# A Trainium2 graph-convolution kernel: embeddings and features of later images through the gather's idle PSUM banks, by halves

## The reference

```python
xn = _gn(x)                                # statistics, then (x - m) / sqrt(v + eps)
emb = einsum('bnc,ec->bne', xn, dist_w)    # 32 numbers per pixel
d2 = sq[:, :, None] + sq[:, None, :] - 2 * einsum('bne,bme->bnm', emb, emb)   # sq: sum of emb squared
adj = (24 nearest by d2) & (dist <= 10) | eye         # 1024 x 1024 zeros and ones
X_lin = xn @ fc_w.T + fc_b                            # features
Dv = sum(adj, axis=2); De = sum(adj, axis=1)
S = (adj / De) @ adj.T / Dv
out = S @ X_lin + xn
o = batchnorm(out)                          # statistics over all four images
result = x + o * sigmoid(o)
```

## Time and profile before

| quantity | value |
|---|---|
| median of 3 runs | 205.23 us (205.18 to 209.13) |
| profiled execution, its own time | 205.92 us |
| its span in the trace | 203.8 us |
| busy share of the span: PE, DVE, ACT, POOL | 87%, 77%, 58%, 42% |
| granted TensorE clock, mean | 0.949 |

### The profile page before, as it was taken

How to read it: one execution, slowest core, us unless ns; L and a number is a source line. 1 busy time by engine, 2 the same in 40 slices (tenths; PEclk the granted TensorE clock), 3 DMA queues, 4 the chain that set the end, 5 groups by cost and what they waited for, 6 DMA issues and landing times.

```text
span 203.8 us, 4396 instructions
## 1 busy us (share of the span) xinstructions
PE 177.9 (87%) x1338; PEld 100.7 (49%) x1338; DVE 156.1 (77%) x912; ACT 118.9 (58%) x207; POOL 85.2 (42%) x120
## 2 busy tenths in 40 slices
PE   7999988889999959999899969999986999999400
PEld 2336352236547636545366645555564577757300
DVE  1789959779998549985995098999999873695664
ACT  2157779687687869637656697444485322060192
POOL 1004821469424169932060689845226751320000
PEclk9999999579999996999999999999999999999955
DMA  5801000155327426422293642442442199610038
GB/s 168 305 5 1 2 3 0 9 99 101 58 54 89 64 6 128 84 53 51 52 60 49 53 106 53 82 77 51 53 56 51 10 125 223 85 30 0 0 115 298
DMA packets 44404, 14.83 MB, mean 73 GB/s; under 512 B 41813, under 2 KB 42453, under 8 KB 44378
## 3 DMA queue, kind: packets, MB, share of 16 engines
q1 hardware_dynamic: 43514, 14.14, 39.4%
q10 hardware_dynamic: 864, 0.40, 0.7%
HBM read 4.02 MB, written 2.13 MB: 30 GB/s over the span
## 4 chain that ended last, share of the span: by engine, by line
PE 36%; DVE 24%; issue 13%; DMA 8%; POOL 8%; ACT 7%; DVEq 2%; SPq 1%; ACTq 0%; POOLq 0%
DVE cand L790 9%; PE pg L366 8%; PE pt L391 7%; PE po L410 6%; PE pt L410 5%; DMA inv_rows<-rdv 5%; POOL H L697 4%; PE pt L431 4%; DVE top L805 3%; DVE cwork L810 3%; DMA dvb<-inv_rows 3%; DVEq L829 2%; DVE xn L992 2%; DVE prod L904 2%; PE pg L343 1%
## 5 line engine op out<-in xcount | busy, mean ns | idle before, releaser
L790 DVE MAX8 cand<-key 128x8 f32<-128x64 f32 x512 | 81.2, 210 | 2.0 <-ACT key L568 1.2
L391 PEld LDWEIGHTS pt<-xp,H 128*128 128x128 bf16 x768 | 45.7, 99 | 22.1 <-issue 14.9
L391 PE MATMUL pt<-xp,H 128*128 128x128 bf16 (+1 forms) x768 | 50.6, 223 | 2.4 <-issue 2.0
L568 ACT ACTIVATE key<-pg 128x512 f32<-128x512 f32 x64 | 35.0, 593 | 26.0 <-PE pg L366 26.0
L366 PE MATMUL pg<-right,left 64*128 64x512 f32 x128 | 47.3, 675 | 3.0 <-ACT key L568 1.4
L576 ACT ACTIVATE sign<-key,thr 128x1024 bf16<-128x1024 f32 x32 | 36.7, 1146 | 11.9 <-DVE thr L816 11.9
L692 POOL TENSOR_SCALAR low<-cs 128x1 f32<-128x1 f32 x32 | 6.0, 187 | 69.7 <-ACT sign L576 66.9
L410 PE MATMUL po<-HT,tp 128*128 128x512 bf16 x144 | 34.0, 380 | 1.1 <-ACT tp L589 0.7
L697 POOL TENSOR_SCALAR H<-sign 128x1024 bf16<-128x1024 bf16 x32 | 33.4, 1043 | 2.5
L366 PEld LDWEIGHTS pg<-right,left 64*128 64x128 f32 x128 | 14.0, 192 | 17.6 <-issue 8.8
L410 PEld LDWEIGHTS po<-HT,tp 128*128 128x128 bf16 x144 | 12.7, 98 | 15.1 <-ACT tp L589 1.2
(11 more groups left out here) (91 smaller groups left out, 199.2 us busy)
## 6 DMA issues: line engine op xcount, KB each, us to landing
out<-xn SPq DMA_DIRECT2D x7, 256.0 KB, 2.1
dvb<-inv_rows SPq DMA_DIRECT2D x3, 512.0 KB, 5.7
x_sb<-x SPq DMA_DIRECT2D x1, 1024.0 KB, 6.2
x_sb<-x SPq DMA_DIRECT2D x1, 512.0 KB, 3.7
HT<-H SPq DMA_TRANSPOSE x32, 3.2
x_sb<-x ACTq DMA_DIRECT2D x1, 256.0 KB, 3.2
x_sb<-x SPq DMA_DIRECT2D x1, 256.0 KB, 3.6
out<-xn SPq DMA_DIRECT2D x2, 128.0 KB, 2.5
```

The costliest lines, as they stand in the source:

```text
L391: mm = pe.matmul(pt[:, j // T_BLOCKS, at:at + wide], lhs, x_cols(b, t, q, wide), start=(t == 0 and j % T_BLOCKS == 0 and q == 0), stop=(t ...
L568: act.activation(key[:, k % KEYS, cols], pg[:, h, :], ACT.Copy).then_inc(s["drained"], 1)
L790: ins = dve.max(cand[:, k % 2, c, :], key[:, k % KEYS, c * CHUNK:(c + 1) * CHUNK])
```

## The change

1. Embeddings and features of images 1 and 2 and the embedding of image 3 (and features of image 0) go through `po` instead of `pg`, with an order of their own (`po_pair`, semaphores `po_filled`, `po_drained`). Features of image 3 stay in `pg`. The embeddings go in steps 0, 5 and 10 (were 1, 6 and 14), their squares' sums in the step behind, `operands` half by half in steps +1 and +2. Features go by halves in steps 3 and 4 (were: 1), 8 and 9 (were: 9) and, image 3's, both in 18 (were: 17).
2. The middle piece of the features moves from ACT to POOL; POOL makes the three pieces of a half in one go (`x_pieces`).
3. The key fill stands first in every step, except t = 3 of images 1 to 3, where the scatter goes first.
4. `gather` of images 0 to 2 goes by piece, then part; it waits for `po_drained` of image 3's embedding. The last image's share of gather(2) is (12, 14, 14, 8) instead of (12, 14, 12, 10).
5. `out_part` moves from t = 7 and t = 4 to t = 1 and t = 2 of the image behind; the statistics `y_stats` of images 0 and 1 move behind the loop: three ahead of the last tile's flag, one behind the last `scale_t`.
6. In the head the statistics of image 2 go behind the operands, those of image 3 behind `candidates(0)`; candidates(0) starts on the first drained half; the group steps of images 2 and 3 move a step later on every engine.

The pieces of the diff stand in the order of the file: tables and `build`, then the loop of PE, the loop of ACT, `x_pieces` on POOL, and DVE.

```diff
+EMB_STEPS = {0: 1, 5: 2, 10: 3}
+X_STEPS = {3: [(1, 0)], 4: [(1, 1)], 8: [(2, 0)], 9: [(2, 1)], 18: [(3, 0), (3, 1)]}
+        po_pair = {("emb", 0): 0, ("x", 0): 1, ("emb", 1): 2, ("x", 1): 3, ("emb", 2): 4, ("x", 2): 5, ("emb", 3): 6}
+        def x_bank(b, h):
+            return (po if ("x", b) in po_pair else pg)[:, h, :]
-                GATHER[b, t] = (b - 1, (12, 14, 12, 10)[t - T_STEP] if b == B - 1 else 8)
+                GATHER[b, t] = (b - 1, (12, 14, 14, 8)[t - T_STEP] if b == B - 1 else 8)
...
+            def gather_order(b):
+                n = len(parts(b))
+                if b == B - 1:
+                    return [(part, q) for part in range(n) for q in range(PIECES)]
+                return [(part, q) for q in range(PIECES) for part in range(n)]
...
+                    if q == 0 and j == 0 and b == 0:
+                        pe.wait_ge(s["po_drained"], 2 * po_pair["emb", B - 1] + part + 1)
...
+                    if b > 0 and t == LAG:
+                        for kk in settled:
+                            scatter(kk)
+                    if k + AHEAD < ALL:
+                        fill_key((k + AHEAD) // TILES, (k + AHEAD) % TILES)
+                    if not (b > 0 and t == LAG):
+                        for kk in settled:
+                            scatter(kk)
+                    if k in EMB_STEPS:
+                        embed(EMB_STEPS[k])
+                    if k - 1 in EMB_STEPS:
+                        norms(EMB_STEPS[k - 1])
+                    for bb, h in X_STEPS.get(k, []):
+                        fill_x(bb, h)
                     if k > 0:
                         flag(k - 1)
+                    if k == 1:
+                        group_variances(2, 2, B)
                     if (b, t) in GATHER:
                         gather(*GATHER[b, t])
...
                     if k > 0:
                         mark(k - 1)
+                    if k == 2:
                         group_sd(2, 2, B)
+                    if k - 2 in EMB_STEPS:
+                        operands(EMB_STEPS[k - 2], 1)
                     if b > 0 and t == T_STEP:
                         t_high(b - 1)
                     if b > 0 and t == T_STEP + 1:
                         t_middle(b - 1)
+                    if k + AHEAD < ALL:
+                        drain_key((k + AHEAD) // TILES, (k + AHEAD) % TILES)
+                    if k in EMB_STEPS:
+                        squares(EMB_STEPS[k])
+                    if k - 1 in EMB_STEPS:
+                        operands(EMB_STEPS[k - 1], 0)
+                    for bb, h in X_STEPS.get(k, []):
+                        drain_x(bb, h)
...
+            def x_pieces(b, h):
+                pool.wait_ge(s["x_hi"], 4 * b + 2 * h + 2)
+                pool.tensor_tensor(x_tiles(xr32, h), x_tiles(x32, h), x_piece(b, h, 0), ALU.subtract)\
+                    .then_inc(s["x_res"], 1)
+                pool.wait_ge(s["x_res"], 2 * b + h + 1)
+                pool.tensor_copy(x_piece(b, h, 1), x_tiles(xr32, h)).then_inc(s["x_mid"], 1)
+                pool.wait_ge(s["x_mid"], 2 * b + h + 1)
+                pool.tensor_tensor(x_piece(b, h, 2), x_tiles(xr32, h), x_piece(b, h, 1), ALU.subtract)\
+                    .then_inc(s["x_lo"], 1)
...
+            dve.wait_ge(s["x_in23"], 16)
+            group_stats(2, 3)
+            group_inverse(1, 1, 2)
+            candidates(0, range(CHUNKS))
             dve.wait_ge(s["step"], group_stats(3, B))
             group_moments(2, B)
...
+                    if b > 1 and t == 1:
+                        out_part(b - 2, 0)
+                    if b > 1 and t == 2:
+                        out_part(b - 2, 1)
...
+            out_part(B - 2, 0)
+            for h in range(2):
+                y_stats(0, h)
+            y_stats(1, 0)
             for k in RELEASE[ALL]:
                 read_flag(k)
                 release(k)
...
             split_last_t(B - 1)
+            y_stats(1, 1)
```

More of the change, by code:

```diff
@@ L182, in build @@
         g_sums = [misc, misc, pt[:, 0, :]]
-        def emb_bank(b, h):
-            return (pg if b > 0 else po)[:, h, :]
         block = ctx.enter_context(nc.Block())
-        first_pairs = [("key", 0, 0), ("key", 0, 1), ("x", 0, 0), ("key", 0, 2), ("key", 0, 3)]
+        first_pairs = [("key", 0, t) for t in range(AHEAD)]
         def pairs_of_step(b, t):
@@ L284, in _ @@
                         inverse_in(b - 1)
[L285 to L288, removed]
+                    for step, image in EMB_STEPS.items():
+                        if image > 1 and b * TILES + t == step + 2 - LAG:
+                            norms_out(image)
+                        if image > 1 and b * TILES + t == step + 3 - LAG:
+                            norms_in(image)
                     if t == TILES - 1 and b < B - 1:
@@ L321, in embed @@
                         pe.wait_ge(s["xn0_ready"], h + 1)
[L322 to L325, removed]
+                    po_free(("emb", b), h)
+                    pe.matmul(po[:, h, :], dW[:, :], xn[:, b, cols], start=True, stop=False,
+                              skip_group_check=True).then_inc(s["po_filled"], 1)
             def norms(b):
@@ L602, in _ @@
             first_operands_end()
-            drain_x(0)
             drain_key(0, 2)
-            x_middle(0)
+            for h in range(2):
+                drain_x(0, h)
             drain_key(0, 3)
@@ L732, in _ @@
                         self_noise(b + 1)
-                    if t == X_STEP + 1 and b + 1 < B:
-                        x_residual(b + 1)
-                    if t == X_STEP + 2 and b + 1 < B:
-                        x_low(b + 1)
+                    for i, (bb, h) in enumerate(X_STEPS.get(k - 1, [])):
+                        if i == 0:
+                            x_pieces(bb, h)
+                    if b == B - 2 and t == TILES - 1:
+                        x_pieces(B - 1, 1)
                     if b > 0 and t == T_STEP:
@@ L953, in _ @@
                         scale_t(b - 1)
-                    if b > 0 and t == TILES - 1:
-                        out_part(b - 1, 0)
-                    if b > 1 and t == T_STEP:
-                        out_part(b - 2, 1)
-                    if b > 1 and t == TILES - 1:
-                        y_stats(b - 2, 0)
-                        y_stats(b - 2, 1)
+            out_part(B - 2, 0)
+            for h in range(2):
+                y_stats(0, h)
+            y_stats(1, 0)
             for k in RELEASE[ALL]:
```

180 lines of the change are left out of this document (66 added, 114 removed).

## The result

| quantity | before | changed |
|---|---|---|
| median of 5 runs each | 206.2 us (205.18 to 209.48) | 196.03 us (195.49 to 200.13) |
| ratio, 95% interval | | 0.9528 [0.9479, 0.9577] |
| profiled execution: own time, span | 205.92, 203.8 | 200.13, 198.1 |
| busy share PE, DVE, ACT, POOL | 87, 77, 58, 42% | 86, 79, 58, 46% |
| mean granted TensorE clock | 0.949 | 0.951 |

The change makes the kernel faster by 4.7%: 196.0 us where 193.3 was forecast (range 189.0 to 200.0). Medians are over all executions, while every ratio leaves out those over 1.5% above the fastest of their kernel. The executions of the changed kernel differ in the granted clock. The median of the eleven is 199.1.

A forecast was written before the change was run, and what follows sets the result against it. DVE sets the pace inside each group of eight tiles and once per image waits for PE to catch up. Terms -6.9 - 5.0 - 0.5 + 0.4 = -12.0 from the 205.23 us median gave 193.3 us, range 189.0 to 200.0.

The forecast's parts named there:

- case A: Whole kernel: the forecast itself, 190.5 to 197 us; chance 0.55.
- Head: Start to the first scale_t: its start moves from 74.11 to 67.2 us, -6.9.
- step (b): Head, DVE: the wait of 2.13 us for gn_sd at 28.12 goes, since the inverse moves a step back.
- PE's sum (35.6 + 28.6 + 3.0): Head: PE's step 4 begins at 35.6, 28.6 us work through scatter(7), 3.0 lost in waits; 67.2.
- Period 2: First to second scale_t: 42.64 us falls to 37.7, -5.0.
- -2.1 in the sum: Period 2: 2.1 us taken off, set against 1.5 for a new wait ahead of the first gather; together -0.6.
- Period 3: Second to third scale_t, 35.15 us before: little left to win, -0.5.
- End: Third scale_t to the end of the span: -0.7 + 0.6 + 0.5 = +0.4 us.
- -0.7 for the wait at the middle piece: End: the wait of 0.73 us at 158.15 goes, as the gather's first sixteen matmuls need no middle piece.
- +0.5 for two gather matmuls: End: two more gather matmuls (2 x 0.23 = 0.46 us) stand ahead of flag(30).
- Case E: Rival: kernel slower through TensorE's clock, shown by a mean clock under 0.8 from 35 to 70 us; chance 0.04.
- case B: Rival: ring only changes its slowest member, 197 to 201 us; signs: thresholds over 4.2 apart, PE waiting behind x_pieces; chance 0.23.

The follow-up runs named there:

- the eleven: All executions of the changed kernel: the five in the result and six from a later repeat without an edit; median 199.1 us.
- e7_inv3: Changed kernel with DVE's group_inverse of images 2 and 3 one tile later; 196.04 us, ratio 0.9514.
- e4_fill: Changed kernel with matmuls of zeros added in PE's three long stands (steps 7, 12 and 28); 195.89 us, ratio 0.9518.
- e2_stats: Changed kernel with the three statistics ahead of the last tile's flag moved to steps 25 (two) and 28 (one); 194.52 us, ratio 0.9451.
- e6_keyfirst: Changed kernel with the key fill ahead of the scatter at t = 3 too, as before the change; 196.88 us, ratio 0.9541.
- e9_xpo: Kernel before the change with only the features of images 1 and 2 going through po; 205.62 us, ratio 0.9977.
- e10_bmid: Kernel before the change with only the middle piece of the features made on POOL; 205.34 us, ratio 0.9979.
- e8_middle: Changed kernel with the middle piece of the features back on ACT; 205.69 us, ratio 1.0008.
- e3_thigh: Changed kernel with ACT's t_high(0) ahead of the second half of image 3's operands in step 12; 195.62 us, ratio 0.9503.
- e11_out: Changed kernel with out_part(1, 1) behind scale_t(2) in step 27 instead of in step 26; 199.22 us, ratio 0.9682.
- e12_best: Changed kernel with earlier statistics, t_high(0) ahead of operands, zero matmuls, and out_part(1, 1) behind scale_t(2), together; 194.41 us, ratio 0.9459.

## Why the prediction was right, and where it was off

**Direction and case.** It was forecast case A, 190.5 to 197, and it came at 196.0. Its miss of 2.7 us can be laid out: 2.0 us are the terms of the table at full clock (+0.9, -0.1, +1.7, -0.5), and the other 0.7 is that the forecast was taken from a median 0.7 below the profiled execution. Two of the terms that came out close did so partly by luck, and the clock had a larger share than the sum gave it.

**Head: direction right, 0.8 us too much.** Features no longer stand in the key ring, PE comes to scatter(7) earlier, DVE's wait for it is 0.85 at full clock. Wrong in it was step (b): the wait for `gn_sd` did not go (2.13, then 2.39). That was harmless, as the times of `e7_inv3` show, because the anchor is set by PE's sum (35.6 + 28.6 + 3.0), and this is the sum that I had used for the number. Inside it two errors nearly cancel. PE's step 4 begins at 37.12 in `e4_fill` and not at 35.6: PE is still at step 3, whose half of image 1's features (1.1 us) the sum had left out. From there to `scale_t` it takes 30.9 us and not 31.6. And I had looked for lost time only behind scatter(0), while the time won lies ahead of it, where before the clock had fallen. The cast on POOL took 0.61 us, where I had taken 0.65:

```profile
22.15 0.61 POOL L673 CAST xp<-xr 128x512 bf16<-128x512 f32 x1
```

The nearest row, half of a 1.193 us operation, comes within 0.02 us of it.

**Period 2: right to 0.1 us at full clock,** 37.63 against 37.7, and that closely by luck. I had added 1.5 for a new wait of PE ahead of the first gather. It is there, 1.70 to 1.92, but it takes the place of the 2.08 for `low`, which I had not taken out: PE's waits in the period sum to 2.85 us before and 2.65 in `e2_stats`. And I had taken out 1.3 for the squares' sums; PE still does those of image 3 (1.06) behind `scale_t(0)`, and in the kernel before it did the same 1.06 in this period. The two errors, 1.7 and 1.3, have opposite signs. The -2.1 in the sum was for the clock. No run shows just that figure; the trace of before shows 2.0 us, in the key fill and the scatter of step 8:

```profile
76.46 2.11 PE L366 MATMUL pg<-right,left 64*128 64x512 f32 x4
78.50 2.60 PE L391 MATMUL pt<-xp,H 128*128 128x129 bf16 x24
81.03 0.19 PE L373 MATMUL misc<-cst,low 128*1 128x1 f32 x2
```

From start to start these take 2.04 and 2.53 us, at a clock of 0.66 over 76 to 81 us; in step 22 they take 1.06 and 1.50. Whether this is won differs by execution: the clock over 76 to 80 us is 1.00 in `e4_fill` and 0.57 in the profiled one, where period 2 is 39.2.

**Period 3: the failed term, 1.7 us.** I wrote that a key fill "goes out of it at the far end" and forgot that the one of the period before comes in at the near end. `e6_keyfirst` puts it back and gets 34.28 us. The rule "scatter first at t = 3" moves two anchors by 0.8 and 1.8 us and leaves the third where it was, since the third is closed by DVE, which waits for the gather before its last three tiles (2.00 us in the profiled execution, 1.03 in `e4_fill`). What exactly holds the gather there is less well settled: PE waits 0.53 and 1.00 us for `low` behind POOL's `x_pieces(3, 0)` ahead of it, and these I did not take away by themselves.

**End: +0.4 forecast, -0.1 measured** in `e4_fill`; the statistics cost 1.3 to 1.8 us for three (`e2_stats`), for which 0.64 for the added one is a fair share. Which of the other two terms (-0.7 for the wait at the middle piece, +0.5 for two gather matmuls) is off by the missing 0.5 I did not separate.

**Clock: a rival in the wrong form.** Case E, slower by TensorE's clock, was to show as a mean under 0.8 from 35 to 70 us. The mean there is 0.95 in the profiled changed execution; before it was 0.90, for the stretch of 36 to 42 us at 0.53, which was missed. What came is three short falls, which are worth 4.3 us of span in an execution that has all of them. They account for times up to some 200.7 us. The execution of 203.78 was not profiled; `e7_inv3` has one of 203.43 with the same mean clock of 0.941, and in that one a further fall (0.50 over 36 to 40 us) and the stop of 2.9 us at `scale_t(0)` come on top.

**Signs of case B.** PE does wait for `low` behind `x_pieces` in the head (1.54, 0.33 and 0.57 us in the trace of the changed kernel), but thresholds 5 to 11 stay under 4.2 us apart (41.74 to 64.85 for six tiles, 3.85 each), so the case did not come.

**The parts don't add.** My sum was made for the change as a whole, along PE, and says nothing of what each part is worth. The features in `po` and the middle piece on POOL, each alone, are worth nothing that can be measured (`e9_xpo` 0.9977, `e10_bmid` 0.9979), and without the middle piece on POOL the rest is worth nothing (`e8_middle` 1.0008). So the middle piece is needed and not enough; which of the other parts must stand beside it was not tested. That taking work off one member of this ring of PE, ACT, DVE and POOL only uncovers the next is what `e3_thigh` and `e7_inv3` suggest.

## What to carry to other kernels

When work is moved past an anchor, book it in both periods: what leaves one enters the other, and only a later anchor tells whether anything was won. When a new wait is added to a sum, take out the old one that stood in its place. In a ring of engines test the parts of a change also by taking one away from the whole; one part alone may show nothing. Look at the executions' clocks, not only at the median, and look for falls of the clock in the kernel before too: they may be part of what a reordering wins.

## What the runs showed of the hardware that I had not expected

The same stand of PE (1.69 us ahead of a key fill) is followed by a granted clock of 0.72 over 54 to 60 us in the changed kernel and of 1.00 in `e2_stats`, which has the same instructions up to step 25. Waits of DVE that the trace puts to "remote" (6.94 us in `e8_middle` and 7.38 in `e7_inv3`, of which 2.5 and 2.9 lie behind the end of the scatter it should be waiting for) and to "issue" (3.09 us in `e11_out`, 2.61 in `e6_keyfirst`) have no cause in these traces. And moving one instruction of 0.69 us on DVE behind the third `scale_t` made the changed kernel about 3 us slower (199.2 against 196.0), while `e12_best` makes the same move and takes 194.4.
